# The additive mask of chunked attention: from products on TensorE into PSUM to copies by ScalarE into PSUM

## What is computed

```python
scores = jnp.einsum('bnqhd,bnkhd->bnhqk', qh, kh) * scale
km = masks[:, 0, :].reshape(N, nc, CHUNK)
scores = scores + jnp.where(km[:, :, None, None, :] > 0, 0.0, NEG)   # NEG = -1e9
attn = jax.nn.softmax(scores, axis=-1)
out = jnp.einsum('bnhqk,bnkhd->bnqhd', attn, vh).reshape(N, T, C)
out = out @ W_out.T + b_out
out = out.transpose(0, 2, 1) * masks
```

## Time and profile before

| | |
|---|---|
| time, median of 3 runs | 1660.42 us (1659.11 to 1662.01) |
| the profiled execution | 1660.06 us, its span 1658.2 us |
| TensorE busy | 1564.0 us (94%) |
| VectorE busy | 1335.9 us (81%) |
| ScalarE busy | 989.7 us (60%) |
| GpSimd busy | 470.9 us (28%) |
| granted TensorE clock | 0.989 of full over the span |

### The profile page before, as it was taken

How to read it: one execution, slowest core, us unless ns; L and a number is a source line. 1 busy time by engine, 2 the same in 40 slices (tenths; PEclk the granted TensorE clock), 3 DMA queues, 4 the chain that set the end, 5 groups by cost and what they waited for, 6 DMA issues and landing times.

```text
span 1658.2 us, 53782 instructions
## 1 busy us (share of the span) xinstructions
PE 1564.0 (94%) x23816; PEld 1311.1 (79%) x23816; DVE 1335.9 (81%) x2006; ACT 989.7 (60%) x1779; POOL 470.9 (28%) x293
## 2 busy tenths in 40 slices
PE   3999999999999999999999999999999999999982
PEld 3888888888888888888888888888888888888872
DVE  1777978879798887978879798887978879798883
ACT  2566576575655666576575656666576575656652
POOL 0113314142232313314142232313314142231313
PEclk9999999999999999999999999999999999999995
DMA  5223232423324233232423314233232423314021
GB/s 212 88 62 103 77 111 66 134 78 115 98 65 128 77 110 104 75 113 66 137 75 116 101 62 128 78 110 103 81 107 69 135 74 116 102 61 128 22 77 51
DMA packets 96182, 158.25 MB, mean 95 GB/s; under 512 B 5328, under 2 KB 38224, under 8 KB 95696
## 3 DMA queue, kind: packets, MB, share of 16 engines
q1 hardware_dynamic: 95952, 154.83, 30.3%
HBM read 121.25 MB, written 33.55 MB: 93 GB/s over the span
## 4 chain that ended last, share of the span: by engine, by line
PE 80%; DVE 12%; ACT 3%; issue 3%; DMA 1%; POOL 1%; SPq 0%; DVEq 0%; POOLq 0%; ACTq 0%
PE pj_ps L278 38%; PE l_ps L278 11%; PE l_ps L382 6%; PE w_ps L313 6%; PE s_ps L302 6%; PE w_ps L331 5%; DVE o_sb L813 2%; PE s_ps L291 2%; PE l_ps L398 2%; PE l_ps L418 2%; ACT o_sb L570 1%; DVE row_max L691 1%; ACT y_hi L521 1%; DVE yt_hl L677 1%; DVE prob L698 1%
## 5 line engine op out<-in xcount | busy, mean ns | idle before, releaser
L895 POOL TENSOR_TENSOR prob<-prob,row_inv 128x1024 f32<-128x1024 f32 x128 | 259.8, 2030 | 980.1 <-DVE row_inv L708 980.1
L580 ACT CAST att_hi<-w_ps 128x256 fp32r<-128x256 f32 x256 | 82.6, 376 | 254.0 <-PE w_ps L331 249.8
L278 PE MATMUL pj_ps<-y_hi,w_hi 128*128 128x512 f32 x512 | 208.5, 407 | 3.7 <-DVE y_lo L673 3.7
L278 PE MATMUL pj_ps<-y_lo,w_hi 128*128 128x512 f32 x512 | 202.5, 395 | 0.0
L278 PE MATMUL pj_ps<-y_hi,w_lo 128*128 128x512 f32 x512 | 202.3, 395 | 0.0
L691 DVE TENSOR_REDUCE row_max<-s_ps 128x16 f32<-128x1024 f32 x128 | 156.0, 1218 | 47.3 <-PE s_ps L302 46.2
L703 DVE TENSOR_REDUCE row_sum<-prob 128x16 f32<-128x1024 f32 x128 | 154.9, 1210 | 45.5 <-ACT prob L562 45.5
L557 ACT COPY prob_t<-w_ps 128x512 f32<-128x512 f32 x256 | 149.8, 585 | 39.3 <-PE w_ps L313 35.7
L313 PE MATMUL w_ps<-cst,prob 128*128 128x128 f32 x1024 | 147.7, 275 | 19.9 <-DVE att_lo L715 19.1
L912 POOL TENSOR_TENSOR o_sb<-o_sb,u_sb 128x1024 f32<-128x1024 f32 x64 | 165.8, 2612 | 1.6 <-ACT o_sb L570 1.6
L698 DVE TENSOR_TENSOR prob<-s_ps,row_max 128x1024 f32<-128x1024 f32 x128 | 155.5, 1215 | 0.1
(11 more groups left out here) (105 smaller groups left out, 3576.0 us busy)
## 6 DMA issues: line engine op xcount, KB each, us to landing
y_raw<-in_ctx SPq DMA_DIRECT2D x64, 512.0 KB, 4.9
yt_raw<-in_ctx_t SPq DMA_DIRECT2D x64, 512.0 KB, 4.1
x_raw<-in_x SPq DMA_DIRECT2D x64, 512.0 KB, 4.8
out_z<-o_sb SPq DMA_DIRECT2D x64, 512.0 KB, 3.4
mask_b<-in_mask SPq DMA_DIRECT2D x64, 256.0 KB, 3.8
u_sb<-in_w SPq DMA_DIRECT2D x1, 2048.0 KB, 10.7
w_sb<-in_w SPq DMA_DIRECT2D x1, 1024.0 KB, 13.7
cst<-in_consts SPq DMA_DIRECT2D x1, 512.0 KB, 5.3
```

The costliest lines, as they stand in the source:

```text
L278: last = mm(dst, lhs, rhs, start=i == 0, stop=i == len(todo) - 1)
L895: nc.gpsimd.tensor_tensor(cut, cut, row_inv[:, u % 2, :].unsqueeze(2).to_broadcast([P, 2 * HEADS, CHUNK]), ALU.mult).then_inc(probs_done, 1)
```

## The change

The mask products of line 291 go. ScalarE copies the mask into the two banks of `s_ps` after `exponents`, for the unit that comes next (`preset_mask(u+1)`: two copies, 128 partitions by 512 float32 each). The 32 score products now all have `start=False` and add onto what ScalarE wrote. `blocked` becomes float32 and holds NEG / SCALE1 or 0, so `flags` multiplies as well. At the start of the program TensorE writes both banks once with an identity product. TensorE waits for `mask_set` where it waited for `shifted` and `blocked_done`; `flags` waits for `mask_set` where it waited for `scores_ready`. The copies to `neg_rows` on VectorE go too.

```diff
                 if e == 0:
                     pe.wait_ge(qkv_copied, count(n, 24, 6 * b + 3))
-                    pe.wait_ge(blocked_done, count(n, 4, b))
-                if exists(n, 8, u - 1):
-                    pe.wait_ge(shifted, count(n, 8, u - 1))
-                for i in range(4):
-                    r, h = divmod(i, 2)
-                    rows = slice(DH * i, DH * i + DH)
-                    mm(s_ps[64 * h:64 * h + 64, r].rearrange("p j g c k -> p j g (c k)"), neg_rows[rows, :],
-                       blocked[rows, b % 2, e * UT:(e + 1) * UT].rearrange("p (j t) -> p j t", j=2).unsqueeze(2).to_broadcast([DH, 2, HALVES, P]),
-                       start=True, stop=False)
-
+                pe.wait_ge(mask_set, count(n, 8, u))
...
-                                      start=False, stop=t == 3 and g == HALVES - 1)
+                                      start=False, stop=True, skip_group_check=True)
...
             pe.wait_ge(weights_in, 5 * 16)
+            for r in range(2):
+                last = mm(s_ps[:, r].rearrange("p j g c k -> p (j g c k)"), ident, cst[:, 0:512], start=True, stop=True)
+            last.then_inc(banks_open, 1)
...
+            def preset_mask(n, u):
+                b, e = divmod(u, 2)
+                if e == 0:
+                    act.wait_ge(blocked_done, count(n, 4, b))
+                if exists(n, 8, u - 1):
+                    act.wait_ge(shifted, count(n, 8, u - 1))
+                else:
+                    act.wait_ge(banks_open, 1)
+                for r in range(2):
+                    last = copy(s_ps[:, r].rearrange("p j g c k -> p j g (c k)"),
+                                blocked[:, b % 2, e * UT:(e + 1) * UT].rearrange("p (j t) -> p j t", j=2).unsqueeze(2).to_broadcast([P, 2, HALVES, P]))
+                last.then_inc(mask_set, 1)
...
             split_y(0, 0)
             split_y(0, 1)
+            preset_mask(0, 0)
...
                     if e == 0:
                         exponents(n, u)
+                        if not (last and u + 1 >= UNITS):
+                            preset_mask(n, u + 1)
...
                 if exists(n, 8, 2 * (b - 2) + 1):
-                    dve.wait_ge(scores_ready, count(n, 8, 2 * (b - 2) + 1))
-                nc.vector.tensor_scalar(blocked[:, b % 2, :], mask_b[:, b % 4, :], 0.0, None, ALU.is_le).then_inc(blocked_done, 1)
+                    dve.wait_ge(mask_set, count(n, 8, 2 * (b - 2) + 1))
+                nc.vector.tensor_scalar(blocked[:, b % 2, :], mask_b[:, b % 4, :], 0.0, NEG / SCALE1, ALU.is_le, ALU.mult).then_inc(blocked_done, 1)
...
-            for i in range(4):
-                last = nc.vector.tensor_copy(neg_rows[DH * i:DH * i + DH, :], cst[0:DH, C_NEG:C_NEG + CHUNK])
-            last.then_inc(neg_done, 1)
```

More of the change, by code:

```diff
@@ L69, in build @@
         mean_mat = cst[:, C_MEAN:C_MEAN + P]
-        neg_rows = sb("neg_rows", [P, CHUNK], BF16)
         w0_sb = sb("w0_sb", [P, 4, HALVES, E])
@@ L94, in build @@
         v_s = sb("v_s", [P, 2, PAIRS, E])
-        blocked = sb("blocked", [P, 2, BT], BF16)
+        blocked = sb("blocked", [P, 2, BT])
         prob = sb("prob", [P, 2, 2, 2, HALVES, P])
@@ L145, in build @@
         weights_in = sem("weights_in")
-        neg_done = sem("neg_done")
+        banks_open, mask_set = sem("banks_open"), sem("mask_set")
         consts_done = sem("consts_done")
```

## The result

The changed kernel takes 1674.91 us (median of 4 runs, 1674.63 to 1675.43) against 1660.82 us for the kernel before (4 runs, 1659.11 to 1662.01). The ratio is 1.009, 95% interval 1.0074 to 1.0105: slower by 0.7% to 1.1%. The forecast was 1663, the range ended at 1672. The profiled execution took 1675.43 us with a span of 1673.7 us, 15.5 us more than the span before (1658.2), at the same mean granted clock of 0.989. One run of the kernel before, in a batch of the experiments, took 2178.51 us at a granted clock of 0.752; no ratio uses it. The mask of the test inputs is 1 everywhere, so the runs show what the copies cost, and not that products add rightly onto other values that ScalarE wrote.

A forecast was written before the change was run, and what follows sets the result against it. TensorE, busy 94% of the span, was taken to bound some slots, with ScalarE or VectorE chains bounding others. 15 x 0.15 - 1.4 + 1.7 = 2.6 us on 1660.06 gave 1662.7, forecast as 1663; range 1654 to 1672.

The forecast's parts named there:

- stall at slot 6 (p): Two ScalarE mask copies of slot 4 delay `copy_pt` and so TensorE in slot 6: 1.0 us, between 0.94 and 1.41.
- gain by a product that counts, 4 a sample: TensorE time between first mask and first score product, saved in slots 0, 4, 8, 14: 0.24 us each.
- lateness at slot 12: Slot 10's copies make `x_hi` 0.21 us late; VectorE, with 0.10 slack, is 0.11 late up to `o_bias`.
- an inner sample: Sum over the even slots of one inner sample: 0.15 us more than before, for 15 samples 2.3 us.
- first sample: No `group_normed` there, so slot 6 has room; 6 of its 8 products count: -1.4 us.
- start: Two opening products on TensorE delay `c1` and the first projections, priced by the t1 products: +1.7 us, once.
- the 154 of the forecast: ScalarE's added busy time: 256 mask copies at about 0.6 us each, 154 us, 60% to 69% of the span.
- rival 4: TensorE's score starts left bare, 0.02 to 0.1 us on 60 slots: +1 to +6 us, up to 1669; 0.15 shared with Rival 3.
- The sign that I gave for it: In the profile, first scores starting over 0.05 us behind their weight loads would show rival 4.
- Rival 1: Delay not paid at slots 6 and 12; five products count, 1.2 us a sample: -17.7 us, 1643; chance 0.15.
- Rival 2: Copies from SBUF to PSUM as dear as `group_normed`, 1.41 us a pair: +14.9 us, 1675; chance 0.1.
- Rival 3: VectorE late after slot 6, products of slots 8 and 14 buy nothing: +7.2 us, 1670; 0.15 shared with rival 4.

The follow-up runs named there:

- the last kernel: Changed kernel with banks opened behind the `c1` products, last `group_normed` moved to slot 6, slot 10's mask copies moved to end of slot 11: 1645.41 us, ratio 0.991.
- e8: Kernel before with `group_normed` in slots 1, 2, 3 and 6 in place of 1 to 4, nothing else changed: 1656.26 us, ratio 0.998.

## Why the prediction was wrong

The mechanism that was forecast is there: the copies of slot 4 delay slot 6, and half of the products count. Four terms of the sum were mis-sized, all in the direction of too fast: the stall a little, and the price of a product, the loss at slot 12 and the start. A fifth was left out.

| term | predicted | measured |
|---|---|---|
| stall at slot 6 (p) | 1.00 | 1.03 |
| gain by a product that counts, 4 a sample | 0.24 | 0.18 |
| lateness at slot 12 | 0.11 | 0.43 |
| an inner sample | +0.15 | +0.74 |
| first sample | -1.4 | -0.75 |
| start | +1.7 | +3.3 (the opening: 2.9) |
| span, in all | +2.6 | +15.5 |

**Right.** The price p, "and I take 1.0": 1.03, paid in full at slot 6. "In slot 6 of 15 samples the first score product waits for `copy_pt` by some 1.2 us": 1.25. "Two copies to `s_ps` of 0.55 to 0.62 us each": 0.60. Which products count: those of slots 0, 4, 8 and 14, while those of 2, 6, 10 and 12 buy nothing; the steps and the kernel without a mask (0.74 a sample, 4 x 0.18) bear that out. "Slot 10's wait for `att_lo` grows by 0.24 to about 1.4": it went from 1.17 in the earlier trace rows to 1.34, by the 0.18 that a product turned out to be worth (timeline of TensorE, slot 10):

```profile
898.05 0.63 PE L303 MATMUL w_ps<-cst,prob 128*128 128x128 f32 x4 [1.34 <-DVE att_lo L724]
```

The copies of slot 8 cost nothing. ScalarE was forecast near 1140 us busy and is at 1111.3: 121.6 more than in the earlier trace rows, 0.95 for each of the 128 pairs of copies. Their records are 0.6 long, but overlap each other and their neighbours, which the 154 of the forecast did not take off.

**Wrong, the price of a product.** "They may show by some 0.02 us; I keep 0.24." With mask products ahead, the weight loads of the scores started 0.22 us ahead of the scores. In the kernel before, slot 10:

```profile
883.50 1.17 PEld L302 LDWEIGHTS s_ps<-k_s,q_s 32*64 32x64 f32 x64
883.72 1.10 PE L302 MATMUL s_ps<-k_s,q_s 32*64 32x64 f32 x64
```

Now loads and scores start together. TensorE in slot 8 of the changed kernel:

```profile
883.39 0.40 PE L277 MATMUL pj_ps<-att_hi,w_lo 128*128 128x512 f32 x1
883.72 1.02 PEld L292 LDWEIGHTS s_ps<-k_s,q_s 32*64 32x64 f32 x64 [0.37 <-issue]
883.72 1.16 PE L292 MATMUL s_ps<-k_s,q_s 32*64 32x64 f32 x64
884.81 0.62 PE L321 MATMUL w_ps<-prob_t,v_s 64*32 64x64 f32 x38
```

The scores take 1.09 us to the next kind of product (883.72 to 884.81), where the earlier trace rows had 1.03 (862.52 to 863.55). It is so in every slot (medians 1.09 and 1.03), and 1.09 without any mask too, where the scores have `start=True`. So 0.06 of the 0.24 come back, on 66 counted slots: 4 us. That was rival 4, and I had set it beside the sum and not in it; a cost with bounds of 0.02 and 0.1 should have gone into the sum at its middle. The sign that I gave for it would not have shown it: the first scores do not start behind their weight loads but with them, and the time is lost inside the group.

**Wrong, slot 12.** The step read "so VectorE is 0.11 late" and "the 0.11 is lost". `x_lo` came 0.17 late (`x_hi` 0.25, against 0.21). But the step took the rest of the chain as rigid. In the kernel before `x_lo` started 0.16 us ahead of GpSimd's scaling (893.41 and 893.57). The scaling starts 4.04 us behind `exp` in all three kernels (889.53 and 893.57, 899.19 and 903.23, 898.67 and 902.71), so a lateness of 0.17 closed the distance and turned the two around. That cost about as much again as the lateness: 0.43 in all, 0.32 over the estimate in each of 16 samples, 5 us.

**Wrong, the start.** I costed the opening at 2048 columns by the t1 products (1.73 us). At the start TensorE ran at half that pace: 3.6 us from the opening's first record to the next product (20.73 to 24.30); the first entry of the clock in this trace turns it to full at 24.64. `c1`'s products were shorter behind it (1.11 us in place of 1.87). So the first projection came 2.9 us later, counted from TensorE's first product, where the sum had 1.7. In this pair of traces the first product stood 0.3 us earlier and the projections ran slow for 0.7 us longer, 3.3 in all. That last 0.7 is in part luck of the draw: the first scores start at 37.8 to 39.0 us in the traces whose program starts as before, and at 40.2 to 41.3 in the five with the opening ahead.

**Left out.** 2.3 us more of waits without a releaser in single samples. The sum held the removal of the mask products to be pure gain, but each of the nine kernels without them loses 3.7 us or more this way, the one without any mask too, and none of the five with them more than 2.3; why is open.

Together: 4 + 5 + 1.6 + 0.5 (p) + 2.3 = 13.4, where the gap between 2.6 and 15.5 is 12.9; the sizes are medians and rounded, and the start is that of one pair of traces.

**The rivals.** Rival 1 (the delay is not paid, 1643) did not happen. The 1645 of the last kernel is near its time by other means, with a product at 0.18 and with two moves that give 4 to 5 us without the change too. Rival 2 (1675) had the right number for a wrong reason: p was 1.03 and not 1.41. Rival 3 did not happen: steps 8-10 and 14-0 are 0.18 shorter, and slots 8 and 14 kept what their products gave. Rival 4 did, at 0.06.

## What to carry to other kernels

Work taken from the busiest engine is worth only what it is worth in the slots where that engine is the limit (here half of them, 10.5 us of 30.7), while work that goes to an engine with spare time on average costs its full length where that engine has no gap. Place such work slot by slot, next to a gap, and not in the same place of every slot: moving two copies, one `group_normed` and the opening turned +14 us into -15, of which 4 to 5 us were to be had without the change. Where a step relies on two engines that start within some tenths of a microsecond of each other on a shared resource, a small lateness can turn their order and cost more than itself.

## What the runs showed of the hardware that was not expected

**The clock at the start, and where its record is missing.** The projections' records take 0.63 us (starts 0.43 apart), where later they take 0.40 (0.23 apart). This slow pace lasts for 3.6 us in the kernel before (26.59 to 30.2), where TensorE had idled 3.68 us, and for 5.7 us in the changed one, idle 3.75. The kernel before with only `group_normed` moved (`e8`) starts by the same program, also idle 3.68, and its slow records last for 5.7 us. So it is not the kernel that sets the length. In the five kernels where TensorE had work until 0.06 to 0.41 us ahead of the projections it lasts 1.4 us at most. Windows of 2 us (length; busy time of TensorE, its weight loads, VectorE, ScalarE, GpSimd; granted clock; DMA share, GB/s), the changed kernel:

```profile
30.00:32.00 2.00, 2.00 (x6) 1.52 (x6) 0.16 (x1) 0.00 (x0) 0.00 (x0) 0.50 0.78 186
...
34.00:36.00 2.00, 2.00 (x8) 1.61 (x7) 0.00 (x0) 0.69 (x1) 0.00 (x0) 0.78 1.05 401
36.00:38.00 2.00, 2.00 (x12) 1.70 (x11) 0.00 (x0) 1.06 (x2) 0.00 (x0) 1.00 0.57 217
```

and the kernel before:

```profile
28.00:30.00 2.00, 2.00 (x6) 1.61 (x5) 0.00 (x0) 0.48 (x1) 0.00 (x0) 1.00 0.83 251
```

In the changed kernel the clock tells the pace: its record has 0.5, the 1.2 GHz level, from 28.05 to 34.88 us, and the last slow record starts at 34.42. The kernel before reads 1.00 with records just as long, but its trace has no entry of the clock ahead of 30.22 us, where it turns to full, and a window without an entry reads 1.00. The last slow record there starts at 29.71. In 12 of the 14 traces the last slow record (over 0.55 us) starts 0.35 to 0.68 us ahead of the entry that turns the clock to full. So where the first tens of microseconds read 1.00, the length of the records tells whether the clock was full or its entry is missing.

**An order decided within some nanoseconds.** The scaling's record starts 5 to 26 ns ahead of `x_lo` in the changed kernel, and `x_lo` is the one that blocks, in all 16 samples. With the copies added to the kernel before, the scaling's record starts 2 to 5 ns ahead in 14 samples, and it is the scaling that blocks; in the other two it starts 20 and 21 ns ahead, and `x_lo` blocks. So the engine whose record starts first need not be the one that goes first, and in a timeline with two decimals the two cases look alike. There the durations tell who waited.
